# A six-layer Perceiver block on one core: new order in four stages, rewritten join to the experts, routing in column tiles

## The reference

```python
inh = sigmoid(x @ Wr / temperature)          # [tokens, 8]
# weights from the distance of inh to 1/e: a zone, or the best two; normalized to sum 1
gate, up = einsum('btd,edf->betf', x, Wg), einsum('btd,edf->betf', x, Wu)
e_out = einsum('betf,efd->betd', silu(gate) * up, Wd)
out = einsum('bte,betd->btd', weights, e_out)
```

## Time and profile before

| what | value |
|---|---|
| median of 3 runs | 3375.05 us (3374.23 to 3379.39) |
| profiled execution, its own time | 3378.06 us |
| its span, first to last instruction | 3376.3 us |
| TensorE matmul busy / share of the span | 3314.9 us / 98% |
| weight loads, VectorE, ScalarE, POOL busy | 2407.1, 2338.4, 1991.2, 1791.5 us |
| chain that ended last | TensorE 59%, DMA 2%, VectorE 1% |
| costliest line of the chain | line 2740, 13% |
| mean granted TensorE clock | 0.994 of full speed |

### The profile page before, as it was taken

One profiled execution on the slowest core, in us unless ns is written; L12 is line 12 of the kernel. 1 busy time (PEld: TensorE's weight loads), 2 busy tenths in 40 slices (PEclk: granted clock), 3 DMA queues, 4 the chain that ended last, 5 costly groups with the idle time before them and its releaser, 6 DMA issues.

```text
span 3376.3 us, 103377 instructions
## 1 busy us (share of the span) xinstructions
PE 3314.9 (98%) x34647; PEld 2407.1 (71%) x34656; DVE 2338.4 (69%) x7546; ACT 1991.2 (59%) x6064; POOL 1791.5 (53%) x3697
## 2 busy tenths in 40 slices
PE   9999999999899999999999999999989999999999
PEld 7888888888666777777777777777756566666665
DVE  5677777777787667888788887878768743444433
ACT  5777777777566557777777777777755411111111
POOL 5666666666566447777777777777746400000000
PEclk9999999999999999999999999999999999999999
DMA  3211111111212241111111111111145710000000
GB/s 98 57 56 54 54 54 57 54 54 54 72 45 64 77 127 45 49 47 46 44 46 49 47 45 45 46 49 47 44 103 154 201 32 19 19 19 19 16 15 6
DMA packets 280200, 187.67 MB, mean 56 GB/s; under 512 B 117037, under 2 KB 276997, under 8 KB 280085
## 3 DMA queue, kind: packets, MB, share of 16 engines
q1 hardware_dynamic: 279797, 185.75, 19.6%
q10 hardware_dynamic: 288, 0.40, 0.1%
HBM read 145.61 MB, written 36.21 MB: 54 GB/s over the span
## 4 chain that ended last, share of the span: by engine, by line
PE 59%; DMA 2%; DVE 1%; issue 0%; ACT 0%; SPq 0%; POOL 0%; DVEq 0%; ACTq 0%; POOLq 0%
PE bank_e L2740 13%; PE c_ps_a L1084 7%; PE bank_e L2717 7%; PE b_ps_a L1050 6%; PE s_ps_a L1057 5%; PE out_ps_a L1110 3%; PE a_ps_a L1061 3%; PE c_ps_a L1061 2%; PE b_ps_a L1061 2%; PE out_ps_a L1094 2%; PE c_ps_a L1143 2%; PE m_ps_r L2335 1%; PE c_ps_a L1122 1%; PE out_ps_a L1181 1%; PE c_ps_a L1133 1%; PE s_ps_r L2343 1%
## 5 line engine op out<-in xcount | busy, mean ns | idle before, releaser
L1210 ACT ACTIVATE probs_a<-s_ps_a,neg_max_a 128x257 f32<-128x257 f32 x1024 | 472.7, 474 | 82.9 <-DVE neg_max_a L1330 78.0
L1264 POOL TENSOR_SCALAR probs_a<-probs_a,gated_a 128x256 f32<-128x256 f32 x1024 | 470.8, 479 | 26.4 <-POOL gated_a L1273 26.4
L1330 DVE TENSOR_REDUCE neg_max_a<-s_ps_a 128x1 f32<-128x257 f32 x1024 | 424.3, 414 | 0.0
L2766 ACT ACTIVATE gate_e<-bank_e 128x512 f32<-128x512 f32 x128 | 76.4, 597 | 493.6 <-PE bank_e L2740 493.5
L530 POOL TENSOR_SCALAR probs_i<-probs_i,inv_sum_i 128x256 f32<-128x256 f32 x512 | 242.8, 487 | 134.7 <-DVE inv_sum_i L694 130.2
L2698 POOL TENSOR_TENSOR inv_std_e<-var_eps_e,half_e 128x4 f32<-128x4 f32 x8 | 8.1, 1009 | 569.6 <-DVE var_eps_e L2780 569.6
L2883 DVE TENSOR_TENSOR hidden_e<-gate_e,bank_e 128x512 f32<-128x512 f32 x128 | 87.4, 688 | 293.8 <-PE bank_e L2740 292.3
L1329 DVE TENSOR_TENSOR self_s_a<-s_ps_a,mask_a 128x32 f32<-128x32 f32 x1024 | 186.1, 182 | 148.1 <-PE s_ps_a L1057 148.0
L514 ACT ACTIVATE probs_i<-s_ps_i,neg_max_i 128x257 f32<-128x257 f32 x512 | 235.9, 473 | 54.5 <-DVE neg_max_i L765 52.8
L372 PE MATMUL a_ps_i<-w_k_i,ctx_t_i 128*128 128x256 f32 x1024 | 252.5, 389 | 5.2 <-issue 5.2
L1084 PE MATMUL c_ps_a<-w_v_a,ctx_t_a 128*32 128x256 f32 x4096 | 247.6, 382 | 0.0
(11 more groups left out here) (394 smaller groups left out, 8202.5 us busy)
## 6 DMA issues: line engine op xcount, KB each, us to landing
ctx_t_i<-in_ctx_t SPq DMA_DIRECT2D x128, 256.0 KB, 2.7
ctx_t_a<-in_ctx_t SPq DMA_DIRECT2D x128, 256.0 KB, 2.7
mask_a<-in_L_xattn_mask SPq DMA_DIRECT2D x512, 4.0 KB, 1.6
v_bd_a<-v_self_a SPq DMA_DIRECT2D x512, 8.0 KB, 1.8
x_tok_i<-in_x SPq DMA_DIRECT2D x32, 128.0 KB, 2.0
x_res_i<-in_x SPq DMA_DIRECT2D x32, 128.0 KB, 2.4
x_after<-y_tok_i SPq DMA_DIRECT2D x32, 128.0 KB, 1.8
x_tok_d<-x_after SPq DMA_DIRECT2D x32, 128.0 KB, 2.3
```

Of the source, the lines that this page charges most:

```text
L1210: act.activation(probs[:, t, :], s_ps[:, g, 0:K], ACT.Exp, bias=neg_max[:, t:t + 1], accum_out=row_sum[:, t:t + 1]).then_inc(exp_done, 1)
L1264: pool.tensor_scalar(probs[:, t, 0:2 * P], probs[:, t, 0:2 * P], gated[:, t:t + 1], 1.0, ALU.mult, ALU.mult).then_inc(probs_ready, 1)
L1330: dve.tensor_reduce(neg_max[:, 4 * f + g:4 * f + g + 1], s_ps[:, g, 0:K], AX.X, ALU.max, negate=True).then_inc(max_ready, 1)
```

## The change

Six things change; the cut of the diff below holds what the steps of the prediction speak of.

- Image: TensorE's slot is split into `project` and `attend`, and the loop's cut lies between them; the order of instructions stays.
- Adapter: slot 0 of each chunk takes slot 1's order (upper half first), on TensorE and ScalarE.
- Reshaped: TensorE's turn is masks, turnings, scores 0, keys 0, scores 1, keys 1, queries, values, four weighings, two outputs. ScalarE copies keys 0 behind the first exponential, keys 1 and queries behind the second. VectorE splits `soften` and puts the sums behind all four normalizations. The last turns have orders of their own.
- Join: SP loads the experts' first rows and constants in turn 5 (`TURNS - 3`), expert 0 at the start of turn 7; VectorE takes their moments and POOL normalizes them in turn 6; TensorE turns two lanes in turn 7 and two in turn 8. The sums of the last turn go into `xn`.
- Routing: `w_route`, padded to 32 columns, stands as weights in four column tiles; the tokens move. VectorE turns the result with one transpose.
- The second half of the last expert's down product ("z") of a turn runs in the next turn, between turnings and routing; the first turn stands ahead of the loop.

```diff
-        every_slot(pe, FIRST + 3, TURNS, slot)
+        for n in range(FIRST + 3, 1):
+            slot(At(n // 4, n % 4))
+        project(At(0, 1))
+        with pe.Fori(0, TURNS) as i:
+            for o in range(1, 5):
+                attend(At(i, o))
+                project(At(i, o + 1))
+        attend(At(TURNS, 1))
+        for n in range(4 * TURNS + 2, B + 1):
+            slot(At(n // 4, n % 4))
...
-                if at.b() == 1:
+                if at.b() in (0, 1):
                     if at.live():
                         pe.wait_ge(turn_read[1][1], at.count(0))
                     turn(a_ps, 0, 1)
...
                 else:
                     pe.wait_ge(turn_read[0][0], at.count(0))
                 turn(b_ps, 0, 0)
...
+            if isinstance(t.i, int) and t.n() == TURNS - 3:
+                sp.wait_ge(stored, 32 * 2)
+                ahead.preload(sp)
...
+            if t.live(1) and not t.live(2):
+                ahead.pool(pool)
...
-                if not t.live(-1):
+                if t.live(1):
                     pe.wait_ge(proj_out["v"], t.done(0, 2))
                     turn_x(pe, t)
+                else:
+                    pe.wait_ge(proj_out["v"], t.done(0, 2))
+                    ahead.first(pe, (0, 1))
+                if not t.live(-1):
                     pe.wait_ge(proj_out["k"], t.done(0, 4))
-                    pe.wait_ge(xt_out, t.done(1, 2))
-                    project_t("k", OUT_BANK)
+                    keys(0)
+                    keys(1)
                 pe.wait_ge(landed["q"], t.done(0, 32))
                 pe.wait_ge(k_spread, t.done(0, 8, 4))
                 pe.sem_inc(pe_waited, 1)
                 score(0)
-            if t.live(1) and t.live(-1):
-                pe.wait_ge(proj_out["v"], t.done(0, 2))
-                turn_x(pe, t)
-            if t.live():
+                if t.live(1) and t.live(-1):
+                    keys(0)
+                if not t.live(1):
+                    pe.wait_ge(y_ready, t.done(-2, LANES, 2))
+                    output(0)
                 pe.wait_ge(k_spread, t.done(0, 8))
                 pe.sem_inc(pe_waited, 1)
                 score(1)
             if t.live(1):
-                if t.live(-2):
-                    pe.wait_ge(y_ready, t.done(-2, LANES))
-                pe.wait_ge(xt_out, t.done(1, 2))
-                if t.live(-1) or not t.live():
-                    project_t("k", OUT_BANK)
-                project_t("q", PROJ_BANK)
-            weigh(0)
+                if t.live() and t.live(-1):
+                    keys(1)
+                if not t.live():
+                    keys(0)
+                    keys(1)
+                for f in range(2):
+                    project_t("q", PROJ_BANK, f)
             if t.live(1):
+                pe.wait_ge(proj_out["q"], t.done(1, 2, 1))
+                values(0)
+                pe.wait_ge(proj_out["q"], t.done(1, 2))
+                values(1)
+                for a in range(LANES):
+                    weigh(a)
                 pe.wait_ge(proj_out["k"], t.done(1, 4))
-            else:
+                output(0)
+                output(1)
+            elif t.live():
                 pe.wait_ge(y_ready, t.done(-2, LANES))
-            output(0)
-            weigh(1)
-            output(1)
-            weigh(2)
-            if t.live(1):
-                pe.wait_ge(proj_out["q"], t.done(1, 2))
-            values(0)
-            weigh(3)
-            values(1)
+                output(1)
+                for a in range(LANES):
+                    weigh(a)
+            elif t.live(-1):
+                pe.wait_ge(y_ready, t.done(-2, LANES, 2))
+                output(0)
+                pe.wait_ge(weighed_out, t.done(-1, LANES, 2))
+                ahead.first(pe, (2, 3))
+                pe.wait_ge(y_ready, t.done(-2, LANES))
+                output(1)
 
...
             exponentials(0)
+            if not second:
+                keys(0)
             exponentials(1)
             if not second:
-                keys(0)
                 keys(1)
-            exponentials(2)
             queries(0)
             queries(1)
+            exponentials(2)
             exponentials(3)
+            values(0)
             if begins:
-                values(0)
                 values(1)
                 turned(0, Turn(0, 0, TURNS))
                 turned(1, Turn(0, 0, TURNS))
             spread(0)
             if not begins:
-                values(0)
+                values(1)
             spread(1)
-            if not begins:
-                values(1)
...
+            if t.live() and not t.live(1):
+                for j in range(2):
+                    add(t, j)
+                    for a in (2 * j, 2 * j + 1):
+                        normalize_weighed(t, a)
+                    for a in (2 * j, 2 * j + 1):
+                        turn_weighed(t, a)
+            elif t.live():
                 normalize_weighed(t, 0)
                 normalize_weighed(t, 1)
-            if not t.live() and t.live(-1):
-                ahead.begin[1](dve)
-            if t.live(-1):
-                add(t, 1)
-            if t.live():
+                turn_values(t, 1, 0)
                 normalize_weighed(t, 2)
                 normalize_weighed(t, 3)
-            if t.live(1):
+                if t.live(-1):
+                    add(t, 0)
+                    add(t, 1)
+                for a in range(LANES):
+                    turn_weighed(t, a)
+                if not t.live(2):
+                    turn_values(t, 1, 1)
+            elif t.live(1):
                 turn_values(t, 1, 0)
-            if t.live():
-                for a in range(LANES):
-                    dve.wait_ge(weighed_out, t.done(0, LANES, LANES - 1 - a))
-                    dve.transpose(attn_t[:, a, :, :].rearrange("p f (g s) -> p g f s", g=G), attn[:, a, :, :, :].rearrange("p g (f c) d -> p g f (c d)", f=2)).then_inc(attn_ready, 1)
+            elif t.live(-1):
+                add(t, 0)
+                add(t, 1)
...
-    ring = Ring([(s, a) for s in ("xT", "r") for a in range(LANES)] + [item for e in range(E) for item in up_down(e)] + [("y", (E - 1) * 2 + n) for n in range(2)])
+    ring = Ring([("xT", a) for a in range(LANES)] + [("z", 0), ("r", 0)] + [None] * 3 + [item for e in range(E) for item in up_down(e)] + [("y", (E - 1) * 2)])
...
+    def first_normalized(pool):
         pool.wait_ge(const_ready, 1)
-        with pool.Fori(0, TURNS) as i:
-            pool.wait_ge(ln_dve, i + 1)
-            pool.tensor_tensor(inv_std[:, :], var_eps[:, :], half[:, :], ALU.pow).then_inc(ln_pool, 1)
+        deviation(pool, 0)
+        pool.wait_ge(ln_pool, 1)
+        for a in range(LANES):
+            pool.tensor_scalar(xn[a][:, :], x_tok[a][:, :], mean_var[:, a, 0:1], inv_std[:, a:a + 1], ALU.subtract, ALU.mult).then_inc(xn_ready, 1)
...
+    def first(pe, lanes):
+        pe.wait_ge(loaded, 16 * 4)
+        for a in lanes:
+            b, _ = ring.place("xT", a)
+            turn_x(pe, 0, a, bank[b], full[b])
...
+        def route(i, w, f):
+            pe.wait_ge(out_of["xT"], ring.out(i, "xT", LANES - 1))
+            for c in range(2):
+                by_block = xn_t[:, c, :].rearrange("p (a s j) -> p s a j", a=LANES, s=4)
+                for s in range(4):
+                    last = pe.matmul(w[32 * s:32 * s + 32, 0:P], w_route[:, c, :], by_block[:, s, :, :], start=c == 0, stop=c == 1)
+            last.then_inc(f, 1)
...
+        pe.wait_ge(*before.high)
+        pe.sem_inc(full[ring.place("z", 0)[0]], 1)
+        b, _ = ring.place("r", 0)
+        route(0, bank[b], full[b])
+        experts(0)
+        with pe.Fori(1, TURNS) as i:
+            for a in range(LANES):
+                turn_x(pe, i, a, *item(i, "xT", a))
+            down(item(i, "z", 0), i, E - 1, 1, back=1)
+            route(i, *item(i, "r", 0))
+            experts(i)
+        b, _ = ring.place("z", 0)
+        held, count = ring.before(TURNS, "z", 0)
+        pe.wait_ge(out_of[held], count)
+        down((bank[b], full[b]), TURNS, E - 1, 1, back=1)
...
-            for a in range(LANES):
-                w = source(i, "r", a)
-                dve.tensor_scalar(neg_z[:, a, :], w[:, 0:E], neg_inv_temp[:, :], EXP_MOST, ALU.mult, ALU.min).then_inc(out_of["r"], 1)
+            link(dve.transpose(z_t[:, :, :].rearrange("p a e -> p (a e)"), source(i, "r", 0)[:, 0:P]))
+            dve.tensor_scalar(neg_z[:, :, :], z_t[:, :, 0:E], neg_inv_temp[:, :], EXP_MOST, ALU.mult, ALU.min).then_inc(out_of["r"], 1)
...
+                final = e == E - 1 and n == 1
+                if final:
+                    b, _ = ring.place("z", 0)
+                    dve.wait_ge(full[b], next_full(i, "z", 0))
+                    w = bank[b]
+                else:
+                    w = source(i, "y", 2 * e + n)
```

198 lines of the change are left out of this document (113 added, 85 removed).

## The result

The changed kernel takes 3339.95 us (median of 4 runs, 3338.35 to 3343.18) for 3375.78 us of the kernel before beside it (4 runs, 3374.23 to 3379.39): 35.8 us less, a ratio of 0.9894 (95% interval 0.9878 to 0.991). The profiled execution took 3341.55 us, its span is 3339.5; the spans differ by 3376.3 - 3339.5 = 36.8 us. The forecast was 3341.5 us.

| part | forecast, us | measured in the traces, us |
|---|---|---|
| image stage | 5.0 | 6.8 |
| adapter stage, slot 0 | 4.5 | 6.7 |
| reshaped stage, up to turn 1 | 3.0 | 1.8 |
| reshaped stage, six steady turns | 6.6 | 5.9 |
| join, last turn's first scores to first gate product | 5.4 | 5.8 |

A forecast was written before the change was run, and what follows sets the result against it. TensorE's stream was taken as the bound. Gains of 5.0 + 4.5 + 3.0 + 6.6 + 5.4 + 9.1 = 33.6 us off 3378.06 gave 3344.5, less 3.0 for the median 3341.5 us; range 3333 to 3353.

The forecast's parts named there:

- The upper end of 5.1 us: Image stage, loop cut moved: best case of the gain, 30 x 0.17 = 5.1 us.
- Rival 2: Image stage: the gap at the loop's cut stays; total gain 28.6 us, time 3346.5 us; chance 0.12.
- The end of 5 us: Adapter stage, slot 0 in the new order: best case of the gain, 5 us, where 4.5 was taken.
- The landing: Reshaped steady turns: the queries' landing, at about 20.7 us, limits a turn as long as TensorE's own 20.8 us.
- its own signs: Reshaped stage: waits for by_dim_q over 0.5 us speak for rival 1; a turn over 21.5 us means wrong.
- rival 1: Queries' landing sets the reshaped turn and the join keeps its stall: gain 25.6 us, time 3349.5 us; chance 0.22.
- rival 4: Reshaped turns: TensorE idles in one piece and the clock falls, 73 us added, time 3414 us; chance 0.03.
- (a): Join: the 3.33 us issue stall in the last scores shrinks with less in the queues; 1.1 us, ends 0 and 3.3.
- (b): Join: the first half of the outputs goes ahead of VectorE's last turnings; 1.8 us.
- (c): Join: of 4.7 us from the outputs' end to the first gate product only routing is left; 4.0 us gained.
- The clock, for which 1.5 us were given back: Join: the clock may fall in TensorE's waits for VectorE; 1.5 us taken off 6.9, leaving 5.4.
- Rival 3: Experts stage: routing does not become shorter; total gain 24.5 us, time 3350.6 us; chance 0.05.

The follow-up runs named there:

- img_cut_back: The changed kernel with TensorE's image-stage loop cut at the slot's start again, as in the kernel before; span 3346.3 us.
- img_cut_mid: The changed kernel with TensorE's image-stage loop cut in the middle of the weighing, 16 records of 64 columns on either side; span 3345.8 us.
- act_q_late: The changed kernel with ScalarE copying the reshaped stage's queries after the third exponentials again, not ahead of them; span 3340.2 us.
- z_first: The changed kernel with the deferred eighth down product ahead of the turning of the next rows in the experts' loop; span 3343.9 us.
- interleave: The changed kernel with weighings and outputs of the reshaped turns interleaved again; span 3342.6 us.

## Why the prediction was right

**Image, 5.0 forecast, 6.8 found.** The place of the edge did it, and the gap did not move along; the size was off, because the row of the wait starts at the modelled end of the last record. Its 0.17 us is a part of the 0.25 us lost at the edge; comparing starts of the same two lines with and without the edge gives the whole, and the length of a pass gives what is left of it, 0.23. The upper end of 5.1 us was too low for the same reason. Rival 2 falls. By the rule of the Trainium skill (Runtime: NRT & Kernel Launch, Instruction fetch mechanics) that the prediction weighed, the gap would have stayed. This trace shows none at the new place, though in img_cut_back and img_cut_mid the edge costs 0.25 to 0.28 us: the measurement decides, and what the gap is made of stays open.

**Adapter, 4.5 and 6.7.** The 0.15 us taken from the outputs' step is there; what was left out is that the first turned group, whose weight loads waited, was itself 0.05 us longer, so that a slot lost 0.20 and not 0.15 us (31 slots, 6.3 us), and that slot 0 of the first chunk, without an output product, lost 0.44 as well. The end of 5 us was again too low.

**Reshaped, first turns, 3.0 and 1.8 (2.3 gained in turn 0, 0.5 lost before it).** act_q_late shows 1.3 to 2.0 us for the earlier copy. The 4.92 us of idle TensorE are gone, but turn 1's scores still run 1.97 us for 1.20, at a granted clock of 0.50 (2516.50 to 2518.50 us).

**Steady turns, 6.6 and 5.9.** 20.8 us was forecast for a turn; 125.4 / 6 = 20.9 is the mean of eight executions, 21.1 this one. TensorE's own turn was mis-sized, 20.8 for the 20.4 us of z_first. The landing was not: in the turn that begins at 2580.71 us the queries' copy ended 10.24 us in, and the next turn's scores followed 10.46 later, 20.7 together as forecast. So the landing is the later of the two limits in most turns, and 2.40 us of waits for it are left in this execution. By its own signs the prediction was not clear of rival 1: two of the five waits for by_dim_q were over 0.5 us (0.62 and 0.93), and three of the six turns over 21.5 (21.98, 21.57 and 21.60). The granted clock was 1.00 over 2520 to 2640 us, so rival 4 did not come. The 0.20 us for a change between whole array and column tiles, with which the sum was made, is borne out by interleave; that agrees with the Trainium skill (TensorEngine Tiling (Array Packing), Key Properties), by which a change of the tiling mode drains the engine. The early copy of the queries has no share in the steady turns that act_q_late could show.

**Join, 5.4 and 5.8.** Right in sum, less so in its terms. (a) 2.0 us of stall went, for 1.1. The prediction took TensorE's stall for the limit; it is VectorE, and the stall counts by what it makes VectorE wait (0.81 us of the 1.34 that are left). (b) and (c) came, and then the wait of 1.87 us for VectorE's attn_t_r took some of it back. The clock, for which 1.5 us were given back, stayed at 1.00 through the join, where it had been 0.63 and then 0.54 in the first gate product: instead of costing 1.5 us it gave 1.7 more, which the table counts to the experts. That it stayed up is luck: seven of the twelve variants lost it in these output products (last section).

**Experts, 9.1 and 9.8.** The 9.8 us are 8.2 of the seven turns, for the 9.1 forecast, and 1.7 of that clock. A turn gained 1.17 us where 1.3 was forecast: the prediction took the length of the routing's row, 1.95 us, whose end is modelled, and to the next group's start it was 1.81. Rival 3 falls: routing takes 0.57 us.

The mechanisms held, and the errors of size have both signs: image and adapter gave 4.0 us more than forecast, the join with the clock behind it 2.1 more, the first turns 1.2, the steady turns 0.7 and the experts' turns 0.9 less. That the sum came within 2 us of the median (3341.5 and 3339.95) is in part luck: the profiled executions differ by 36.5 us, 2.9 more than the sum, while the median lies 1.6 us under the profiled execution after, where 3.0 were taken.

## What to carry to other kernels

Price a gap per pass by the distance between starts of the same two groups with and without it, not by the wait's own row; in a loop of thirty passes the rest came to a third more. Where a stage repeats, the length of a pass is surer than its end: 27.39 us in eleven executions whose ends lay 3.5 us apart. Try a loop's back edge behind long records (here no gap was left), and put a wait behind work that does not need it. At a join, look for the engine that is back to back there, which need not be the one that bounds the stages on both sides, and take work off it; but look at the granted clock of what follows before you count the gain.
